# Second attention's value products in bursts of four key blocks, with six score banks and rows of three pairs

## The chip, the cores and the metric

The kernel runs on one core of a Trainium2 chip. The metric is the device time of one execution in microseconds; the median of the runs is compared. TensorE (PE) multiplies matrices, VectorE (DVE) and ScalarE (ACT) work element by element, GpSimd (POOL) does simple element work, and SyncE (SP) issues the DMAs. Each engine takes its own list of instructions in order and meets the others at semaphores.

## The reference

Sixteen sequences of 512 tokens with 128 features go through two layers. Each layer normalises, and adds an attention and a feed-forward product to its input:

```
xn = layernorm(x);  x = x + attn0(xn) + ffn0(xn)     # layer 0: 16 heads of 64, causal, with slopes
xn = layernorm(x);  x = x + attn1(xn) + ffn1(xn)     # layer 1: differential attention
# attn1, for each of 8 heads, with two query/key sets of 8 features and values of 16:
o1 = softmax(q1 k1^T * 8**-0.25) @ v;  o2 = softmax(q2 k2^T * 8**-0.25) @ v
o  = rmsnorm(o1 - lam * o2) * w + b;   attn1 = (1 - lambda_init) * concat(o) @ Wo^T
```

The change is in attn1's products `softmax(...) @ v`: 8 heads x 2 sets = 16 score sets, in 4 groups (`NG`) of 4 (`GS`), each over 4 key blocks of 128 (`NT`).

## The kernel before

All engines walk through the same clock of *ticks*. A sequence takes 32 ticks (`TICKS`), four for each of the first layer's 8 head pairs; what an engine does in a tick depends on the tick modulo 4 (`r`) and is an order written out by hand in each engine's `tick`. Each piece of work has a tick of its own (`FA_AT`, `WOB_AT`, ...). The first layer of one sequence runs beside the second layer of the sequence before: in a tick TensorE projects q, k or v of a pair, makes scores (`max_scores0`, L1500), turns probabilities (`turn_probs`, L1517) or multiplies them with the values (`pv0`, L1532), and between them it does *steps* of the second attention. There are 46 steps (`NU + KEY_LAG`) in 28 ticks, so one or two in a tick, its `part` 0 and 1.

A step of the second attention makes two score tiles for the row maxima (`second_tops`, L1605, read by DVE's `row_max1`, L1250) and, 14 steps later, two score tiles with the keys as rows (`second_keys`, L1591); ACT's `exp1` (L989) writes the exponentials of the latter to `pt1`. Two tiles are a *unit*; 8 units are a group. `pt1` holds two blocks of four tiles, used in turn. Every second step `second_values` runs `pv1` (L1552 to L1563) for one key block: 4 heads' matmuls, recorded as 8, into the bank `op`. After the fourth block ACT copies `op` to `oraw` (`copy_heads`, L973, at step 9 of the group's end), TensorE turns `oraw` (`turn_heads`, step 10), and DVE and POOL normalise (`head_norm_a`, `head_scale`, `head_norm_b`). The fourth group's last block, copy and turn have ticks of their own (`TAIL_AT`, `TURN3_AT`). In the clock modulo 32 the fourth blocks of the groups stand in ticks 7, 12, 17 and 22.

TensorE's eight result banks are two for projections (`pj`), five for scores (`sc`, `SCB`) and `op`. Projections of all kinds take the two `pj` banks in turn, in the order that `pj_order` lists; `bank` makes TensorE wait until the use two before has been read. Score tiles take the score banks in turn in the order of `score_order`; `bank_free` makes TensorE wait for the reader of the tile that had the bank. Tick 12 also holds `WOB_AT`: the second half of the first layer's output projection (L1548, 128 matmuls), and tick 13 begins with the last turning of a pair and its `pv0`.

The first layer's probabilities stand in `pq`, four pairs deep (`NROWS`); DVE writes a pair when the pair four before has been turned. In the last sequence parts of `pq` serve as the second attention's stacks, values and result.

Of the kernel before, what the change touches and what calls it, by code (L numbers as in the profile page):

```python
# [55 lines left out]
NROWS = 4  # L56
# [58 lines left out]
L1_TICKS = 28  # L115
# [28 lines left out]
KEY_LAG = 14  # L144
# [6 lines left out]
PV_LAG = (0, 0)  # L151
L1_STEPS = NU + KEY_LAG
SCB = 5


def l1_chunk(h, part=None):

    m = (h - L1_AT) % TICKS
    steps = range(L1_STEPS * m // L1_TICKS, L1_STEPS * (m + 1) // L1_TICKS) if m < L1_TICKS else range(0)
    return steps if part is None else steps[part:part + 1]  # L160
# [22 lines left out]
def l1_heads(t, at, last=NG - 1):  # L183

    g, r = divmod(t - KEY_LAG - at, GU)
    return g if r == 0 and 0 <= g < last else None
# [5 lines left out]
               (TURN3_AT, f"o{NG - 1}"), (OT_AT, "oT"), (OUT_AT, "wo1")]  # L192
# [3 lines left out]
class Seq:  # L196
# [21 lines left out]
    def live(self):  # L218

        return 0 <= self.lo < NB  # L220

# [23 lines left out]
def l1_steps(h, k, part=None):  # L245

    steps = []
    for n, clock in enumerate((h, k)):
        if clock is not None:
            i = Seq((clock - L1_AT) // TICKS)  # L250
            if i.live() and i.last() == (n == 1):
                steps.extend((i, t) for t in l1_chunk(clock, part))
    return steps
# [22 lines left out]
def pj_order():  # L276
# [3 lines left out]
    def second(h, k, part):  # L280

        for i, t in l1_steps(h, k, part):
            if (group := l1_rows(t)) is not None:
                order.append((f"n{group}", i.lo))
            if (group := l1_heads(t, TURN_AT[i.last()])) is not None:
                order.append((f"o{group}", i.lo))

# [11 lines left out]
    for g, h, k in clocks():  # L299
# [3 lines left out]
        if late(g) and r == 0:  # L303
# [4 lines left out]
            second(h, k, 1)  # L308
        elif late(g) and r == 1:
            pairs("pv", g, 3)  # L310
            second(h, k, 0)
            misc(g, h, k)
            second(h, k, 1)
        elif late(g) and r == 2:
# [3 lines left out]
            second(h, k, 1)  # L318
        elif late(g) and r == 3:
            second(h, k, 0)  # L320
            misc(g, h, k)
            second(h, k, 1)
        elif r == 0:
            pairs("q", g, -1)
            pairs("k", g, -1)
            second(h, k, 0)
            second(h, k, 1)
            misc(g, h, k)
        elif r == 1:
# [3 lines left out]
            misc(g, h, k)  # L333
        elif r == 2:
            second(h, k, 0)
            pairs("v", g, -1)
            misc(g, h, k)
            second(h, k, 1)
        else:
            second(h, k, 0)  # L340
            misc(g, h, k)
            second(h, k, 1)
# [3 lines left out]
def score_order():  # L346
# [3 lines left out]
    def second_keys(h, k, part):  # L350

        for i, t in l1_steps(h, k, part):
            if t >= KEY_LAG:
                order.extend(("st1", 2 * (t - KEY_LAG) + n, i.lo) for n in range(2))

# [128 lines left out]
def build_program(nc, a, out):  # L484
    ctx = ExitStack()
    with ctx:
# [73 lines left out]
        stacks = [(QS, KS), tuple(rows_of[n][:, 0:H1 * T // 2].bitcast(BF16).rearrange("p (n t) -> p n t", n=H1) for n in range(2))]  # L560
# [3 lines left out]
        result = [xres, rows_of[3][:, 0:NT * D].rearrange("p (t d) -> p t d", t=NT)]  # L564
        values1 = [v1, rows_of[2][:, 0:NT * H1 * 32].rearrange("p (t h e) -> p t h e", t=NT, h=H1)]
        pt1 = sb("pt1", [P, 2 * GS, T])
# [11 lines left out]
        ow = sb("ow", [P, NT, 2, DV])  # L578
# [4 lines left out]
        op = ps("op")  # L583
# [37 lines left out]
        s_or = sem("heads_copied")  # L621
# [9 lines left out]
        flat = pt1[:, :, :].rearrange("p a f -> p (a f)").rearrange("p (n f) -> p n f", f=2 * FF)  # L631
# [48 lines left out]
        def _(sp):  # L680
# [36 lines left out]
            def stack(i, w):  # L717
# [5 lines left out]
                if i.last():  # L723

                    sp.wait_ge(s_tr, i.upto(N_TURN, 6 * 6))
# [36 lines left out]
        def _(pool):  # L762
# [10 lines left out]
            def last_stacks(i):  # L773

                pool.wait_ge(s_tr, i.upto(N_TURN, 6 * 6))
                pool.memset(stacks[1][1][:, :, :], 1.0).then_inc(s_pset, 1)
                pool.wait_ge(s_tr, i.upto(N_TURN, 6 * 7))
# [31 lines left out]
            def scale_probs(i, p, q):  # L809

                for c in (2 * q, 2 * q + 1):
                    j, row = ROWS[c]
                    at = PT0 * (2 * (p % NROWS) + j) + ROW_OFF[row]
# [4 lines left out]
                    pool.tensor_scalar(rows, rows, rsum[:, p % NROWS, c:c + 1], None, ALU.mult).then_inc(s_scl, 1)  # L818
# [11 lines left out]
            def small(g, h, k):  # L830
# [6 lines left out]
                for i, t in l1_steps(h, k):  # L837
                    if (group := l1_heads(t, TURN_AT[i.last()] + SCALE_LAG[i.last()])) is not None:
# [40 lines left out]
        def _(act):  # L879
# [62 lines left out]
            def exp0(i, p, q):  # L942

                for c in (2 * q, 2 * q + 1):
                    j, row = ROWS[c]
                    at = PT0 * (2 * (p % NROWS) + j) + ROW_OFF[row]
                    rows = pq[:, at:at + P * (row + 1)]
                    act.wait_ge(s_mxd0, i.upto(L0N, 8 * p + c + 1))
                    act.activation(rows, rows, ACT.Exp, scale=-1.0, bias=mx0[:, p % NROWS, c:c + 1],  # L949
                                   accum_out=lsum[:, p % NROWS, c:c + 1]).then_inc(s_exp0, 1)  # L950
# [31 lines left out]
            def exp1(i, n):  # L982

                m, j = divmod(n, GS // 2)
                if j == 0:
                    hold(act, s_pv1, i.upto(NG * NT, m - 1))
                for h in range(2):
                    act.wait_ge(s_st1, i.upto(L1N, 2 * n + h + 1))
                    act.activation(pt1[:, GS * (m % 2) + 2 * j + h, :], sc[tile_bank(i, "st1", 2 * n + h)][:, :],  # L989
                                   ACT.Exp, scale=float(DS) ** -0.25).then_inc(s_exp1, 1)  # L990

            def second_attention(h, k, part):

                for i, t in l1_steps(h, k, part):
                    if (group := l1_rows(t)) is not None:
                        minus_max1(i, group)
                    if (group := l1_heads(t, HEADS_AT[i.last()])) is not None:
                        copy_heads(i, group)
                    if t >= KEY_LAG:
                        exp1(i, t - KEY_LAG)  # L1000

            def others(g, h, k):
# [12 lines left out]
                for i in second_at(h, k, VALS_AT):  # L1015
# [7 lines left out]
                    else:  # L1023
                        hold(act, s_pv1, i.upto(NG * NT, 0))
# [76 lines left out]
        def _(dve):  # L1101
# [80 lines left out]
            def row_max0(i, p, q):  # L1182
# [4 lines left out]
                for c in (2 * q, 2 * q + 1):  # L1187
# [3 lines left out]
                    at = PT0 * (2 * (p % NROWS) + j) + ROW_OFF[row]  # L1191
                    left = P if row == 1 else 0
                    scores_there = i.upto(6 * NPAIR, m + 1)
                    if i.first():
# [4 lines left out]
                                             op0=ALU.add, op1=ALU.min, accum_out=mx0[:, p % NROWS, c:c + 1]).then_inc(s_mxd0, 1)  # L1199

            def invert_sums(i, p, q):

                dve.wait_ge(s_exp0, i.upto(L0N, 8 * p + 2 * q + 2))
                dve.reciprocal(rsum[:, p % NROWS, 2 * q:2 * q + 2], lsum[:, p % NROWS, 2 * q:2 * q + 2]).then_inc(s_rc, 1)  # L1204
# [79 lines left out]
            def second_attention(h, k, part):  # L1284

                for i, t in l1_steps(h, k, part):
                    if (group := l1_rows(t)) is not None:
                        minus_max1_rest(i, group)
                    if (group := l1_heads(t, TURN_AT[i.last()] + NA_LAG[i.last()])) is not None:
# [546 lines left out]
```

## Time and profile before

| | |
|---|---|
| runs shown | 2510.09, 2512.21, 2514.51 us; median 2512.21 us |
| profiled execution | 2513.58 us, of which the span from the first to the last instruction is 2511.6 us |
| busy share of the span | PE 94%, PE weight loads 44%, DVE 74%, ACT 75%, POOL 57% |
| granted TensorE clock | 0.986 of full speed, mean |

The span has a start of some 170 us in which the first sequence has nothing beside it, 15 sequences whose second layer runs beside the next one's first, and an end from about 2400 us on. Times in the timeline are from the span's start. A busy PE is not PE at its peak, since matmuls overlap and their ends are modelled; so block costs are read from one start to the next.

### The profile page before, as it was taken

How to read it: one execution, taken by the hardware profiler on the slowest of the kernel's cores; microseconds unless marked ns; L12 is line 12 of the kernel's file. 1: busy time of each engine (PE TensorE's matmuls, PEld its weight loads, DVE VectorE, ACT ScalarE, POOL GpSimd, SP SyncE). 2: the span in 40 equal slices, each digit the busy share in tenths (PEclk: the TensorE clock that was granted, in tenths of full speed). 3: DMA queues.
4: the chain of work that ended last, by engine and by line, in shares of the span. 5: the costliest groups of instructions: out<-in, count | busy, mean ns of one | idle time of the engine just before them, and what ended most of it. 6: DMA issues, size and time to landing. Idle time of an engine off the chain costs nothing.

```text
span 2511.6 us, 81917 instructions
## 1 busy us (share of the span) xinstructions
PE 2370.6 (94%) x32896; PEld 1112.7 (44%) x32896; DVE 1856.1 (74%) x5637; ACT 1882.8 (75%) x4707; POOL 1430.7 (57%) x1356
## 2 busy tenths in 40 slices
PE   6999999999999999999999999999999999999886
PEld 2454444444444444444444444444444444444421
DVE  4558777777877778777777877778777776867675
ACT  4866787878778777787878778777787878778545
POOL 5866474665656556474665656556574655646311
PEclk8999999999999999999999999999999999999978
DMA  3002020200202002020200202002020200202020
GB/s 96 7 14 45 3 61 3 49 15 7 57 2 57 6 19 44 3 61 3 53 10 7 56 3 61 3 21 43 7 56 3 55 8 7 57 3 56 2 56 5
DMA packets 59944, 70.43 MB, mean 28 GB/s; under 512 B 11056, under 2 KB 55344, under 8 KB 56368
## 3 DMA queue, kind: packets, MB, share of 16 engines
q1 hardware_dynamic: 59568, 65.21, 11.5%
q8 instruction: 262, 4.29, 0.7%
q14 instruction: 114, 0.93, 0.1%
HBM read 35.04 MB, written 29.36 MB: 26 GB/s over the span
## 4 chain that ended last, share of the span: by engine, by line
PE 72%; ACT 14%; DVE 10%; issue 2%; DMA 1%; POOL 1%; SPq 0%; POOLq 0%; ACTq 0%; DVEq 0%
PE pj L1436 17%; PE pj L1532 10%; PE sc L1500 9%; PE op L1561 7%; PE sc L1517 7%; ACT pt L989 5%; PE pj L1548 5%; PE pj L1456 5%; DVE mx L1250 4%; PE sc L1605 4%; PE sc L1591 4%; ACT pq L949 3%; ACT pt L967 3%; PE pj L1426 3%; DVE pq L1197 2%
## 5 line engine op out<-in xcount | busy, mean ns | idle before, releaser
L818 POOL TENSOR_SCALAR pq<-pq,rsum 128x128 f32<-128x128 f32 (+3 forms) x1024 | 1130.5, 1121 | 743.0 <-DVE rsum L1204 742.6
L1250 DVE TENSOR_REDUCE mx<-sc 128x1 f32<-128x512 f32 x1024 | 655.9, 683 | 199.1 <-PE sc L1605 195.1
L989 ACT ACTIVATE pt<-sc 128x512 f32<-128x512 f32 x1024 | 556.3, 610 | 191.5 <-PE sc L1591 191.2
L949 ACT ACTIVATE pq<-pq,mx 128x128 f32<-128x128 f32 (+3 forms) x1024 | 573.2, 576 | 16.6 <-DVE mx L1197 16.6
L967 ACT ACTIVATE pt<-sc 128x512 f32<-128x512 f32 (+1 forms) x768 | 360.8, 538 | 221.2 <-PE sc L1517 217.7
L1197 DVE CUSTOM_DVE_ANT_0 pq<-sc,relkey 128x128 f32<-128x128 f32 (+3 forms) x1024 | 448.3, 484 | 104.9 <-PE sc L1500 100.0
L1500 PE MATMUL sc<-K,Q 64*128 64x128 f32 (+3 forms) x2048 | 365.5, 454 | 26.9 <-ACT pt L989 16.7
L1532 PE MATMUL pj<-pt,v 128*32 128x512 f32 (+3 forms) x4096 | 304.5, 438 | 3.9 <-ACT y L917 0.6
L1517 PEld LDWEIGHTS sc<-ident,pq 64*128 64x128 f32 x5120 | 199.2, 139 | 171.6 <-issue 127.3
L1436 PE MATMUL pj<-xnT,wqkv 128*32 128x512 f32 x2048 | 264.4, 609 | 7.6 <-DVE xres L1173 2.9
L1561 PE MATMUL op<-pt,v 128*32 128x512 f32 x1920 | 256.8, 607 | 2.2 <-ACT pt L989 2.0
L1517 PE MATMUL sc<-ident,pq 64*128 64x64 f32 x5120 | 234.8, 228 | 24.4 <-DVE mx L1197 12.8
L1500 PEld LDWEIGHTS sc<-K,Q 64*128 64x128 f32 x2048 | 159.8, 188 | 153.5 <-issue 133.6
L1605 PE MATMUL sc<-KS,QS 48*128 48x512 bf16 x960 | 210.2, 384 | 16.9 <-ACT pt L967 5.5
L949 ACT ACTIVATION_READ_ACCUMULATOR pq<-pq,mx 128x1 f32 x1024 | 220.1, 215 | 0.0
L1591 PE MATMUL sc<-QS,KS 51*128 51x512 bf16 x960 | 199.9, 386 | 6.0 <-ACT pt L967 4.2
L1532 PEld LDWEIGHTS pj<-pt,v 128*32 128x32 f32 x4096 | 126.1, 110 | 160.8 <-issue 134.2
L1591 PEld LDWEIGHTS sc<-QS,KS 51*128 51x128 bf16 x960 | 51.0, 94 | 226.4 <-issue 119.7
L1605 PEld LDWEIGHTS sc<-KS,QS 48*128 48x128 bf16 x960 | 58.0, 94 | 190.4 <-DVE mx L1250 60.6
L1436 PE MATMUL pj<-wqkv,xnT 128*32 128x128 f32 x4096 | 138.9, 276 | 0.0
L1436 PEld LDWEIGHTS pj<-wqkv,xnT 128*32 128x32 f32 x4096 | 104.6, 110 | 55.2 <-issue 52.0
L1204 DVE RECIPROCAL rsum<-lsum 128x2 f32<-128x2 f32 x512 | 79.4, 155 | 58.6 <-ACT pq L949 58.3
(117 smaller groups left out, 2798.2 us busy)
## 6 DMA issues: line engine op xcount, KB each, us to landing
scr_p<-y SPq DMA_DIRECT2D x160, 128.0 KB, 2.4
QS<-scr_p SPq DMA_DIRECT2D x30, 384.0 KB, 6.1
KS<-scr_p SPq DMA_DIRECT2D x30, 384.0 KB, 8.8
x_in<-in_L_attn_x SPq DMA_DIRECT2D x16, 256.0 KB, 2.8
scr_p<-tanh SPq DMA_DIRECT2D x32, 128.0 KB, 2.4
out_x<-xres SPq DMA_DIRECT2D x15, 256.0 KB, 2.3
QS<-nrow SPq DMA_DIRECT2D x180, 4.0 KB
wqkv<-in_L_attn_w_qkv SPq DMA_DIRECT2D x1, 1536.0 KB, 6.5
```

Source lines behind the costliest of these rows:

```text
L818: pool.tensor_scalar(rows, rows, rsum[:, p % NROWS, c:c + 1], None, ALU.mult).then_inc(s_scl, 1)
L949: act.activation(rows, rows, ACT.Exp, scale=-1.0, bias=mx0[:, p % NROWS, c:c + 1], accum_out=lsum[:, p % NROWS, c:c + 1]).then_inc(s_exp0, 1)
L967: act.activation(to[:, :, h, :], sc[tile_bank(i, "tr0", m)][:, 0:cols].rearrange("p (n c) -> p n c", c=HALF), ACT.Copy).then_inc(s_ev, 1)
L989: act.activation(pt1[:, GS * (m % 2) + 2 * j + h, :], sc[tile_bank(i, "st1", 2 * n + h)][:, :], ACT.Exp, scale=float(DS) ** -0.25).then_in ...
L1197: dve.tensor_tensor_reduce(out=pq[:, at:at + width], in0=sc[tile_bank(i, "mx0", m)][:, left:left + width], in1=relkey[:, T - width:T], sca ...
L1250: dve.reduce_max(mx1[:, g % 2, at:at + 1], sc[tile_bank(i, "mx1", 2 * t + h)][:, :], AXIS.X).then_inc(s_mxd1, 1)
L1436: last = pe.matmul(t[r, c * k:c * (k + 1)], w(k)[:, r], x(k), start=True, stop=True)
L1500: last = pe.matmul(sc[tile_bank(i, "mx0", m + j)][:, left:left + width], Q0[r, b, P * row:P * (row + 1)], K0[r, b, 0:width], start=True, s ...
L1517: last = pe.transpose(sc[tile_bank(i, "tr0", m + h)][:, HALF * n:HALF * (n + 1)], pq[r, at:at + P], ident[r, r])
L1532: last = pe.matmul(t[r, P * k:T], v0[:, p % NBUF, k, r], pt[:, base:base + WIDTH[k]], start=k == 0, stop=k == NT - 1)
L1561: last = pe.matmul(op[32 * j:32 * (j + 1), :], values1[i.last()][:, k, (GS * g + j) // 2, :], pt1[:, GS * (k % 2) + j, :], start=k == 0, s ...
L1605: pe.matmul(sc[tile_bank(i, "mx1", 2 * t + n)][:, :], queries[r, slot, P * q:P * (q + 1)], keys[r, slot, :], start=True, stop=True).then_i ...
```

## The change

`pv1` no longer runs block by block. It runs once for a group, at step 8 after the group's first keys (`VALUES_AT`; the place of the fourth block before), as one burst of four key blocks, into a `pj` bank under the name `w0` to `w3`; inside it TensorE waits before each block for that block's exponentials. `copy_heads` reads that `pj` bank. The bank `op` is gone and there are six score banks. `pt1` grows from 8 tiles to 9 units (18 tiles), used in turn through all sequences; `exp1` waits for the block that last read the unit. `NROWS` goes from 4 to 3, with pairs counted through all sequences (`row_slot`), `ow` becomes another name of `dif`, and the last sequence's stacks, values and result move to other rows. The orders of the engines' ticks stay; `pj_order` gets `values` where TensorE's order had `second_values`. `L1_TICKS` and `KEY_LAG` become pairs with the same values.

```diff
-NROWS = 4
+NROWS = 3
+UNITS = 9
-PV_LAG = (0, 0)
-SCB = 5
+VALUES_AT = (8, 8)
+SCB = 6
...
+def row_slot(i, p):
+    return i.upto(NPAIR, p) % NROWS
...
 SECOND_MISC = [..., (FB_AT, "fb"),
-               (TURN3_AT, f"o{NG - 1}"), ...]
+               (TAIL_AT, f"w{NG - 1}"), (TURN3_AT, f"o{NG - 1}"), ...]
...
+    def values(h, k, part):
+        for i, t in l1_steps(h, k, part):
+            if (group := l1_heads(i, t, VALUES_AT[i.last()])) is not None:
+                order.append((f"w{group}", i.lo))
...
         elif r == 0:
             pairs("q", g, -1)
             pairs("k", g, -1)
+            values(h, k, 0)
             second(h, k, 0)
+            values(h, k, 1)
             second(h, k, 1)
             misc(g, h, k)
...
-        pt1 = sb("pt1", [P, 2 * GS, T])
+        pt1 = sb("pt1", [P, 2 * UNITS, T])
-        ow = sb("ow", [P, NT, 2, DV])
+        ow = dif
-        op = ps("op")
...
             def copy_heads(i, g):
-                act.wait_ge(s_pv1, i.upto(NG * NT, NT * (g + 1)))
-                act.activation(oraw[:, :], op[:, :], ACT.Copy).then_inc(s_or, 1)
+                b, u = pj_use(i, f"w{g}")
+                act.wait_ge(s_pjf[b], u)
+                act.activation(oraw[:, :], pj[b][:, :], ACT.Copy).then_inc(s_pje[b], 1)
...
             def exp1(i, n):
-                m, j = divmod(n, GS // 2)
-                if j == 0:
-                    hold(act, s_pv1, i.upto(NG * NT, m - 1))
+                unit = i.upto(NU, n)
+                if unit >= UNITS:
+                    was, m = divmod((unit - UNITS) // (GS // 2), NG * NT)
+                    group, k = divmod(m, NT)
+                    if k < NT - 1:
+                        act.wait_ge(s_pv1, Seq(was).upto(NG * (NT - 1), (NT - 1) * group + k + 1))
+                    else:
+                        b, u = pj_use(Seq(was), f"w{group}")
+                        act.wait_ge(s_pjf[b], u)
...
-            def pv1(i, g, k):
-                pe.wait_ge(s_exp1, i.upto(L1N, GS * (NT * g + k + 1)))
-                if k == 0:
-                    hold(pe, s_or, i.upto(NG, g))
-                    ...
-                for j in range(GS):
-                    last = pe.matmul(op[32 * j:32 * (j + 1), :], values1[i.last()][:, k, (GS * g + j) // 2, :],
-                                     pt1[:, GS * (k % 2) + j, :], start=k == 0, stop=k == NT - 1)
-                last.then_inc(s_pv1, 1)
+            def pv1(i, g):
+                ...
+                t, full = bank(i, f"w{g}")
+                for k in range(NT):
+                    pe.wait_ge(s_exp1, i.upto(L1N, GS * (NT * g + k + 1)))
+                    for j in range(GS):
+                        unit = i.upto(NU, (GS * (NT * g + k) + j) // 2)
+                        last = pe.matmul(t[32 * j:32 * (j + 1), :], values1[i.last()][:, k, (GS * g + j) // 2, :],
+                                         pt1[:, 2 * (unit % UNITS) + j % 2, :], start=k == 0, stop=k == NT - 1)
+                    if k < NT - 1:
+                        last.then_inc(s_pv1, 1)
+                last.then_inc(full, 1)
...
             def second_values(h, k, part):
                 for i, t in l1_steps(h, k, part):
-                    m = t - KEY_LAG
-                    if m >= GS // 2 + PV_LAG[i.last()] and (m - PV_LAG[i.last()]) % (GS // 2) == 0:
-                        pv1(i, *divmod((m - PV_LAG[i.last()]) // (GS // 2) - 1, NT))
+                    if (group := l1_heads(i, t, VALUES_AT[i.last()])) is not None:
+                        pv1(i, group)
...
                 for i in second_at(h, k, TAIL_AT):
-                    pv1(i, NG - 1, NT - 1)
+                    pv1(i, NG - 1)
```

## Rows read from the trace of the kernel before

**Rows 1.** The page's first part: busy us (share of the span) x instructions, by engine.

```profile
PE 2370.6 (94%) x32896; PEld 1112.7 (44%) x32896; DVE 1856.1 (74%) x5637; ACT 1882.8 (75%) x4707; POOL 1430.7 (57%) x1356
```

**Rows 2.** The page's chain that ended last, by engine, by line.

```profile
PE 72%; ACT 14%; DVE 10%; issue 2%; DMA 1%; POOL 1%; SPq 0%; POOLq 0%; ACTq 0%; DVEq 0%
PE pj L1436 17%; PE pj L1532 10%; PE sc L1500 9%; PE op L1561 7%; PE sc L1517 7%; ACT pt L989 5%; PE pj L1548 5%; PE pj L1456 5%; DVE mx L1250 4%; PE sc L1605 4%; PE sc L1591 4%; ACT pq L949 3%; ACT pt L967 3%; PE pj L1426 3%; DVE pq L1197 2%
```

**Rows 3.** Windows: length, busy of PE, PEld, DVE, ACT, POOL, then clock, DMA.

```profile
1307.82:1323.35 15.53, 15.14 (x178) 5.55 (x176) 10.75 (x32) 13.78 (x36) 8.09 (x8) 1.00 0.01 2
1323.35:1350.61 27.26, 26.25 (x375) 12.26 (x373) 21.44 (x61) 21.23 (x53) 12.78 (x13) 1.00 0.01 3
1350.61:1355.11 4.50, 4.50 (x139) 3.70 (x138) 1.46 (x5) 0.59 (x2) 4.50 (x4) 1.00 0.02 4
1355.11:1375.88 20.77, 19.86 (x237) 8.77 (x234) 14.18 (x64) 19.14 (x51) 11.39 (x14) 1.00 0.05 16
1375.88:1397.43 21.55, 21.44 (x284) 9.12 (x286) 17.25 (x46) 18.59 (x48) 15.15 (x14) 1.00 0.24 66
1397.43:1458.25 60.82, 58.41 (x865) 29.52 (x857) 50.29 (x146) 43.92 (x110) 36.71 (x36) 1.00 0.19 36
sum 150.43, PE 145.60 PEld 68.91 DVE 115.36 ACT 117.26 POOL 88.63; mean PE 24.27 PEld 11.49 DVE 19.23 ACT 19.54 POOL 14.77
```

**Rows 4.** Groups by line, value matmuls: count, busy us, mean ns, idle before.

```profile
L1561 PE MATMUL op<-pt,v 128*32 128x512 f32 x1920 | 256.8, 607 | 2.2 <-ACT pt L989 2.0
```

**Rows 5.** Timeline of PE: start us, length us, line, tiles, count.

```profile
1215.96 1.92 PE L1436 MATMUL pj<-xnT,wqkv 128*32 128x512 f32 x16
1217.82 0.39 PE L1591 MATMUL sc<-QS,KS 51*128 51x512 bf16 x2
...
1393.38 0.39 PE L1591 MATMUL sc<-QS,KS 51*128 51x512 bf16 x2
1393.70 1.06 PE L1561 MATMUL op<-pt,v 128*32 128x512 f32 x8
1394.70 0.39 PE L1591 MATMUL sc<-QS,KS 51*128 51x512 bf16 x2
1394.92 0.81 PE L1500 MATMUL sc<-K,Q 64*128 64x384 f32 x4
```

**Rows 6.** Timeline of PE behind the second output projection; in brackets idle time before.

```profile
1355.11 0.39 PE L1591 MATMUL sc<-QS,KS 51*128 51x512 bf16 x2
...
1355.67 2.36 PE L1532 MATMUL pj<-pt,v 128*32 128x512 f32 x32
...
1359.21 0.92 PE L1500 MATMUL sc<-K,Q 64*128 64x384 f32 x4 [0.64 <-ACT pt L989]
```

**Rows 7.** Timeline of ACT in the same place.

```profile
1355.59 1.09 ACT L989 ACTIVATE pt<-sc 128x512 f32<-128x512 f32 x2 [4.38 <-PE sc L1591]
...
1357.96 0.61 ACT L973 ACTIVATE oraw<-op 128x512 f32<-128x512 f32 x1
1358.44 1.11 ACT L989 ACTIVATE pt<-sc 128x512 f32<-128x512 f32 x2
```

**Rows 8.** Windows of ACT alone inside stretches 2 and 4: length, busy, clock, DMA.

```profile
1332.80:1339.29 6.49, 6.32 (x17) 1.00 0.00 1
1355.59:1375.20 19.61, 18.46 (x49) 1.00 0.06 16
```

**Rows 9.** PE's waits from 1247 to 1308: us in total, times, longest (first and last).

```profile
PE sc L1500 <- DVE mx L1250: 0.7, 1, 0.7
...
PE pj L1436 <- DVE xres L1173: 0.2, 1, 0.2
```

**Rows 10.** Timeline of PE near 173 us, and the windows view just behind.

```profile
173.04 0.46 PE L1517 MATMUL sc<-ident,pq 64*128 64x64 f32 x8 [2.29 <-DVE mx L1197]
173.44 4.05 PE L1532 MATMUL pj<-pt,v 128*32 128x512 f32 x32
...
173.94:177.36 3.42, 3.42 (x32) 1.16 (x24) 0.90 (x7) 1.13 (x5) 3.42 (x4) 0.50 0.00 0
```

More of the change, by code:

```diff
@@ L150, with l1_chunk @@
 NA_LAG = (0, 0)
-PV_LAG = (0, 0)
-L1_STEPS = NU + KEY_LAG
-SCB = 5
-def l1_chunk(h, part=None):
+VALUES_AT = (8, 8)
+SCB = 6
+def l1_chunk(h, last, part=None):
     m = (h - L1_AT) % TICKS
-    steps = range(L1_STEPS * m // L1_TICKS, L1_STEPS * (m + 1) // L1_TICKS) if m < L1_TICKS else range(0)
+    ticks, all_steps = L1_TICKS[last], NU + KEY_LAG[last]
+    steps = range(all_steps * m // ticks, all_steps * (m + 1) // ticks) if m < ticks else range(0)
     return steps if part is None else steps[part:part + 1]
@@ L251, in l1_steps @@
             if i.live() and i.last() == (n == 1):
-                steps.extend((i, t) for t in l1_chunk(clock, part))
+                steps.extend((i, t) for t in l1_chunk(clock, n, part))
     return steps
@@ L352, in second_keys @@
         for i, t in l1_steps(h, k, part):
-            if t >= KEY_LAG:
-                order.extend(("st1", 2 * (t - KEY_LAG) + n, i.lo) for n in range(2))
+            if t >= KEY_LAG[i.last()]:
+                order.extend(("st1", 2 * (t - KEY_LAG[i.last()]) + n, i.lo) for n in range(2))
     def second_tops(h, k, part):
@@ L837, in small @@
                 for i, t in l1_steps(h, k):
-                    if (group := l1_heads(t, TURN_AT[i.last()] + SCALE_LAG[i.last()])) is not None:
+                    if (group := l1_heads(i, t, TURN_AT[i.last()] + SCALE_LAG[i.last()])) is not None:
                         head_scale(i, group)
@@ L996, in second_attention @@
                         minus_max1(i, group)
-                    if (group := l1_heads(t, HEADS_AT[i.last()])) is not None:
+                    if (group := l1_heads(i, t, HEADS_AT[i.last()])) is not None:
                         copy_heads(i, group)
-                    if t >= KEY_LAG:
-                        exp1(i, t - KEY_LAG)
+                    if t >= KEY_LAG[i.last()]:
+                        exp1(i, t - KEY_LAG[i.last()])
             def others(g, h, k):
@@ L1288, in second_attention @@
                         minus_max1_rest(i, group)
[L1289 removed]
+                    if (group := l1_heads(i, t, TURN_AT[i.last()] + NA_LAG[i.last()])) is not None:
                         head_norm_a(i, group)
[L1291 removed]
+                    if (group := l1_heads(i, t, TURN_AT[i.last()] + NORM_LAG[i.last()])) is not None:
                         head_norm_b(i, group)
@@ L1576, in second_turns @@
                         pe.transpose(rows[0:16, 0:P], mx1[:, group % 2, 0:16], ident[:, :]).then_inc(full, 1)
-                    if (group := l1_heads(t, TURN_AT[i.last()])) is not None:
+                    if (group := l1_heads(i, t, TURN_AT[i.last()])) is not None:
                         turn_heads(i, group)
```

77 lines of the change are left out of this document (46 added, 31 removed).

## The prediction

> **What bounds the kernel now.** I read the busy line first: TensorE 94% of the span, ACT and DVE 75% each [rows 1]. That alone would say that any time taken off TensorE comes off the end. The chain of waits says less: 72% of the span runs over TensorE, 14% over ACT, 10% over DVE, and the value matmuls (L1561) hold 7% of it, 176 us, where they are busy 257 us in 15 of the 16 sequences alone [rows 2, 4]. About a third of their time is beside the path already. So I cut one steady sequence (150.43 us) into six stretches at the value blocks that the change touches and read which engine has room in each [rows 3]: TensorE has none anywhere, but ACT is busy 13.78 of 15.53 us in stretch 1, 19.14 of 20.77 in stretch 4 and 18.59 of 21.55 in stretch 5. Inside them it runs without a break: 6.32 of 6.49 us and 18.46 of 19.61 us [rows 8]. In such places a shorter TensorE only waits for ACT.
>
> **The sum, per sequence.** There are 15 sequences of this shape: 1920 matmuls by 8 a block are 240 blocks, 16 each [rows 4]. The sixteenth sequence, at the end, is priced by itself.
>
> *What a block and a burst cost.* A block of 8 matmuls takes 1.00 us from its start to the next start, and the key scores in front of it take 0.32 instead of 0.22, so a removed block is worth 1.10. Sixteen matmuls of the same kind in a row take 1.86, so each further eight costs 0.86 [rows 5]. A burst is then 1.00 + 3 x 0.86 = 3.58 us where its last block was 1.00: 2.58 longer. By TensorE alone a sequence gains 12 x 1.10 = 13.2 and pays 4 x 2.58 = 10.3: 2.9 us. Between the four parts of a burst stands a wait for exponentials; if each part paid a full 1.00 again, a burst would be 0.42 longer (1.7 us a sequence).
> The Trainium skill ("TensorEngine Tiling (Array Packing)", Key Properties) says that a change of tiling mode drains the engine; by that rule the 2.9 us would simply be gained, which is the first rival below. The same page (PSUM Bottleneck) warns that packing speeds up TensorE but not the emptying of its banks; ACT's rows bear that out here.
>
> *Stretch 1 (1307.82 to 1323.35), three blocks gone.* TensorE alone: -3.3. ACT's idle time is 1.75, and the burst must wait for the exponentials of its last unit, behind that same ACT queue. Between 0 and -1.75; I take -1.2, nearer to ACT's end, since TensorE's own saving is twice that.
>
> *Stretch 2 (to 1350.61), a burst in, three blocks gone.* +2.6. The two blocks ahead of the first FFN's second product lie where ACT runs 6.32 of 6.49 us on end [rows 8] and the next key scores need banks that ACT still reads; I let them give 1.1 of 2.2. The third stands before DVE work and gives its 1.1. Net +0.4, between -0.7 (all given) and +2.6.
>
> *Stretch 3 (to 1355.11), a burst in.* The group's last block is followed at once by the 128 matmuls of the output projection; ACT works 0.59 us in it [rows 3], nothing covers it: +2.6.
>
> *Stretch 4 (to 1375.88), the new wait.* The projection banks are handed out in turn, two of them. In this tick the uses become q, k, **w1** (the burst), woB, and then pv of the next tick, so pv needs the bank of w1, that is, ACT's copy_heads. Before, its bank was k's. TensorE reaches pv at 1355.67, right after woB [rows 6]; but ACT gets to copy_heads only at 1357.96 and ends it at 1358.57, because ahead of it in ACT's queue stand the exponentials whose keys TensorE issues after woB (1355.59), the two turned copies and the first layer's exponentials [rows 7]. TensorE stops for 2.9 us, and queued behind pv are the key scores that ACT takes next (1357.96, now some 2.9 later): both engines lose it. The three blocks of this stretch cannot pay for it: ACT's work cannot shrink and its idle time is 19.61 - 18.46 = 1.15 [rows 8], of which I let 0.7 go, since the next pv comes behind ACT's copies again. So +2.2, between +1.75 and +2.9.
>
> *Stretch 5 (to 1397.43), a burst in, three blocks gone.* TensorE alone +2.6 - 3.3 = -0.7; ACT has 2.96 us of room [rows 3], but its copy now waits for the end of the burst: I take -0.6, between -0.7 and +1.
>
> *Stretch 6 (to 1458.25), a burst in and the sixth score bank alone.* +2.6 for the last group's burst. TensorE's six waits in the same place one sequence before, from 0.7 for DVE's maxima to 0.2 for DVE's residual, make 1.9 [rows 9]; with one tile more in the ring each asks for the reader of a tile earlier, so I count them all gone, though one is for a projection bank: +0.7, between +0.7 and +2.6, or lower if shorter stalls inside blocks go too (to -1).
>
> Together -1.2 + 0.4 + 2.6 + 2.2 - 0.6 + 0.7 = **+4.1 us** a sequence, some 60 us over 15 (61.5, less a little for the first and last of them, whose neighbours differ).
>
> *Edits that I cost at nothing.* Rows of three pairs: DVE's first scores of a pair now wait for the turning of the pair three before it, which program order has 3 ticks earlier, 3 x 150.43 / 32 = 14 us [rows 3]; that is the cover, and without it the price is a DVE wait of what is missing. Nine units of pt1: a unit needs the buffer of the one nine before, first at step 9, where ACT already waits for the whole burst in copy_heads. In the last sequence copy_heads comes a step later and that wait stands alone; there ACT also loses its keys during a burst but has no value blocks between its units; I put its tail at 0, between -5 and +5 us (two bursts' 2.6 either way). ow in dif: both are DVE's, in order. SP's and POOL's waits on turned pairs move in the last sequence alone, to pairs turned 5 ticks or more before; the number of DMAs is the same. After w0 the next use, q, takes the bank of ya3, which is empty by then; k takes w0's and waits for its copy a little, which is inside stretch 2's bounds.
>
> The profiled execution took 2513.6 us; 2513.6 + 60 = 2573.6. The median of the runs shown is 1.4 lower, so I forecast **2572 us**.
>
> **Rivals.**
> *TensorE alone decides (faster).* Its 94% and 72% speak for it. Then every removed block counts: -2.9, the sixth bank -1.9, and pv's wait +2.9, which no bank order here removes: -1.9 a sequence, 28 us, **2484 us**. It decides where ACT's queue would be more than 2 us ahead of TensorE in stretches 1, 2 and 4; rows 8 speak against it. That ACT could reach copy_heads before woB ends, so that pv does not wait at all, would add 2.9 (2440 us); exponentials whose keys come after woB stand before it, so I give that almost nothing.
> *The clock falls after the new wait (slower still).* After TensorE stood still for 2.29 us at 173.04, pv0's 32 matmuls took 4.05 us instead of 2.36, at a granted clock of 0.50, which is 1.2 GHz [rows 6, 10]. The new wait is longer than that one and pv follows it. That costs up to 1.7 more a sequence, 25 us: **2597 us**. Against it: it is one row, and not every sequence need meet it.
> The Trainium skill ("TensorE: Matmul & The Clock Gate", Part 1) says that the engine's default state is the throttled one and that activity releases it; the row agrees.
> *The gains and the waits cancel.* If stretches 1 and 2 give what their bounds allow (-1.75 and -0.7) and stretch 6 gives -1, the sum is +1.5, and 1.5 us more from stretch 4 or 5 would make it nothing: **2512 us**.
>
> **How the numbers follow.** Forecast 0.52 (its own range 2545 to 2595), clock 0.20, TensorE alone 0.18, cancelled 0.10. A difference under 0.2%, 5 us, is no change here. The cancelled case splits about evenly over faster, same and slower, and the others fall on their sides: faster 0.20, same 0.06, slower 0.74. The range takes in the clock case with part of the burst's bound (2615) above, and below it the better ends of stretches 1, 2 and 6, which reach to 2505; about 0.13 of the chance lies under it and 0.06 above.
>
> **What would show it.** Right: a wait of some 2.9 us on TensorE before L1532 for ACT's copy into oraw, once in a sequence, and as long an idle time on ACT before the next key exponentials; bursts of 32 matmuls of 3.5 to 3.6 us; the 0.64 us wait of L1500 for L989 behind pv gone [rows 6]; TensorE's busy time some 45 us lower (15 x 2.9) while its idle time grows by some 100; ACT's busy time unchanged. Wrong: a wait for that copy under 1 us; stretch 4 no longer than before; or TensorE's idle time not above its 2511.6 - 2370.6 = 141 us [rows 1]. If bursts take 4.0 us, the price of a part was wrong, not the reason.

## The result, and the profile after

| | before | after |
|---|---|---|
| median of 4 runs, us | 2511.15 (2507.31 to 2514.51) | 2625.36 (2623.81 to 2630.20) |
| ratio | | 1.0459, 95% interval 1.0438 to 1.0479 |
| span of the profiled execution, us | 2511.6 | 2623.7 |
| granted TensorE clock, mean | 0.986 | 0.974 |

The change makes the kernel 4.6% slower. The direction and the new wait came as forecast; the time did not: 2625 lies 10 us above the range and 53 above the forecast.

The page's busy line and chain of the kernel after, to be read beside [rows 1, 2]:

```profile
PE 2383.2 (91%) x32896; PEld 1163.5 (44%) x32896; DVE 1848.2 (70%) x5637; ACT 1870.9 (71%) x4707; POOL 1426.6 (54%) x1356
PE 67%; ACT 17%; DVE 10%; issue 4%; POOL 1%; DMA 0%; SPq 0%; POOLq 0%; ACTq 0%; DVEq 0%
```

ACT's and DVE's busy times are within 12 us of those before. TensorE's idle time went from 141 to 240 us, as forecast (some 100 more). Its busy time did not fall by 45 us, it rose by 13. The chain now runs 17% over ACT. Where TensorE waits (whole run: us in total, times, longest; the first five rows of after):

```profile
PE pj L1568 <- ACT oraw L1000: 41.7, 14, 3.0
PE sc L1553 <- ACT pt L1023: 23.0, 28, 1.5
PE pj L1598 <- ACT v L960: 17.4, 14, 1.2
PE sc L1631 <- DVE mx L1233: 13.2, 43, 0.7
PE pj L1472 <- ACT Q L949: 12.4, 14, 0.9
```

The first row is the predicted one (2.98 us each, 2.9 forecast). The third, group 3's burst waiting for ACT's copy of v, was not predicted. The second is new in its length: before, the same turns (L1517) waited 28 times for these exponentials, 0.2 us at the longest and 5.9 in all, while 16.7 us of waits for them stood before L1500; those are gone. One sequence of after in windows (length, busy of PE, PEld, DVE, ACT, POOL, clock, DMA), from group 3's burst of the sequence before: stretches 6 and 1 together, then 2, 3, 4 and 5 of [rows 3]:

```profile
1288.12:1364.00 75.88, 72.77 (x1034) 35.83 (x1034) 61.09 (x177) 56.76 (x143) 44.75 (x43) 1.00 0.15 29
1364.00:1391.59 27.59, 26.45 (x375) 12.81 (x374) 20.97 (x61) 20.83 (x53) 12.39 (x13) 1.00 0.01 3
1391.59:1398.65 7.06, 7.06 (x160) 4.47 (x161) 1.44 (x5) 0.92 (x2) 5.50 (x4) 1.00 0.01 2
1398.65:1423.51 24.86, 19.25 (x213) 9.56 (x210) 14.16 (x65) 19.07 (x51) 10.30 (x13) 0.93 0.04 13
1423.51:1446.55 23.04, 20.91 (x283) 9.43 (x283) 17.24 (x46) 19.03 (x49) 15.36 (x14) 1.00 0.20 54
sum 158.43, PE 146.44 PEld 72.10 DVE 114.90 ACT 116.61 POOL 88.30; mean PE 29.29 PEld 14.42 DVE 22.98 ACT 23.32 POOL 17.66
```

Nearly all the growth is in stretches 3 to 5, and stretch 4 alone has a clock below 1. TensorE's and then ACT's timeline there (start, length, line, tiles; in brackets idle time before and what ended it), where [rows 6, 7] stood before:

```profile
1391.59 3.64 PE L1598 MATMUL pj<-pt,v 128*32 128x512 f32 x32 [0.19 <-ACT Q L949]
1395.04 3.68 PE L1584 MATMUL pj<-wout,att 128*32 128x128 f32 x128
1398.65 0.39 PE L1631 MATMUL sc<-QS,KS 51*128 51x512 bf16 x2
1398.88 0.41 PE L1553 MATMUL sc<-ident,pq 64*128 64x64 f32 x8
1402.26 4.05 PE L1568 MATMUL pj<-pt,v 128*32 128x512 f32 x32 [2.98 <-ACT oraw L1000]
1406.25 0.39 PE L1631 MATMUL sc<-QS,KS 51*128 51x512 bf16 x2
...
1406.69 0.81 PE L1536 MATMUL sc<-K,Q 64*128 64x384 f32 x4
```

```profile
1399.14 1.09 ACT L1023 ACTIVATE pt<-sc 128x512 f32<-128x512 f32 x2 [6.63 <-PE sc L1631]
...
1401.51 0.61 ACT L1000 ACTIVATE oraw<-pj 128x512 f32<-128x512 f32 x1
1406.73 1.08 ACT L1023 ACTIVATE pt<-sc 128x512 f32<-128x512 f32 x2 [4.61 <-PE sc L1631]
```

The burst takes 3.45 us from its start to the next start. `pv0` stands 2.98 us until ACT's copy, which stands behind exponentials whose keys came after the output projection, and ACT then idles 4.61 us for its next keys. The 0.64-us wait of [rows 6] is gone. `pv0` itself takes 4.05 us instead of 2.36, at half the clock (1.2 GHz), as a window inside it shows:

```profile
1402.73:1406.14 3.41, 3.41 (x32) 1.51 (x24) 0.00 (x0) 0.00 (x0) 0.00 (x0) 0.50 0.00 0
```

And in stretch 5, the wait that was missed, with the projection before it:

```profile
1437.40 1.92 PE L1472 MATMUL pj<-xnT,w_l 128*32 128x512 f32 x16 [0.89 <-ACT Q L949]
...
1446.55 3.64 PE L1598 MATMUL pj<-pt,v 128*32 128x512 f32 x32 [1.24 <-ACT v L960]
```

Over twelve steady sequences (the second to the thirteenth), from burst start to burst start (medians, us):

| stretch | before | after | change | forecast |
|---|---|---|---|---|
| 6 and 1 | 76.38 | 75.89 | -0.5 | -0.5 |
| 2 | 27.01 | 27.60 | +0.6 | +0.4 |
| 3 | 4.49 | 7.07 | +2.6 | +2.6 |
| 4, clock at 1.00 (4 of 12) | 20.77 | 23.16 | +2.4 | +2.2 |
| 4, clock at 0.50 in part (8 of 12) | 20.77 | 24.3 to 25.5 | +3.6 to +4.8 | (a rival) |
| 5 | 21.55 | 23.04 | +1.5 | -0.6 |

### The profile page after: what moved, and what is told of

Its sections match the earlier page's. It is cut to its first block, busy times and chain, and to the rows that moved or that the text cites. A ratio compares the mean times of both kernels' runs of the same rounds, so it can differ in the third digit from the quotient of the medians.

```text
span 2623.7 us, 82166 instructions
## 1 busy us (share of the span) xinstructions
PE 2383.2 (91%) x32896; PEld 1163.5 (44%) x32896; DVE 1848.2 (70%) x5637; ACT 1870.9 (71%) x4707; POOL 1426.6 (54%) x1356
## 4 chain that ended last, share of the span: by engine, by line
PE 67%; ACT 17%; DVE 10%; issue 4%; POOL 1%; DMA 0%; SPq 0%; POOLq 0%; ACTq 0%; DVEq 0%
PE pj L1472 16%; PE pj L1568 12%; PE pj L1598 9%; ACT pt L1023 9%; PE sc L1536 6%; PE sc L1553 5%; DVE mx L1286 5%; PE pj L1584 5%; PE pj L1492 4%; PE sc L1631 4%; PE sc L1645 4%; ACT pq L975 4%; PE pj L1462 2%; ACT pt L993 2%; DVE pq L1233 2%
## 5 line engine op out<-in xcount | busy, mean ns | idle before, releaser
L1568 PE MATMUL pj<-pt,v 128*32 128x512 f32 (+3 forms) x4096 | 321.4, 457 | 44.4 <-ACT oraw L1000 41.7
L1598 PE MATMUL pj<-pt,v 128*32 128x512 f32 x1920 | 218.4, 595 | 25.5 <-ACT v L960 17.4
L1631 PE MATMUL sc<-QS,KS 51*128 51x512 bf16 x960 | 217.7, 386 | 18.8 <-DVE mx L1233 13.2
L1568 PEld LDWEIGHTS pj<-pt,v 128*32 128x32 f32 x4096 | 134.6, 114 | 210.1 <-issue 182.2
L813 POOL TENSOR_SCALAR veps<-mv 128x4 f32<-128x4 f32 x64 | 15.0, 234 | 240.0 <-DVE mv L1186 236.2
L851 POOL TENSOR_SCALAR mse<-ms 128x8 f32<-128x8 f32 x64 | 13.1, 205 | 227.8 <-DVE ms L1304 225.4
```

The lines of the kernel that those rows point to most:

```text
L1568: last = pe.matmul(t[r, P * k:T], v0[:, p % NBUF, k, r], pt[:, base:base + WIDTH[k]], start=k == 0, stop=k == NT - 1)
L1598: last = pe.matmul(t[32 * j:32 * (j + 1), :], values1[i.last()][:, k, (GS * g + j) // 2, :], pt1[:, 2 * (unit % UNITS) + j % 2, :], start= ...
L1631: pe.matmul(sc[tile_bank(i, "st1", 2 * m + n)][:, :], keys[r, slot, P * k:P * (k + 1)], queries[r, slot, :], start=True, stop=True).then_i ...
```

## The experiments

My theory on seeing this: three terms make up the miss, the wait for v's copy, the clock behind the new wait, and something small at the end. Rivals: ScalarE is late whatever task asks (then a wait removed turns up elsewhere); the clock falls for another reason; the bursts cost more by themselves than the forecast allowed, and the sixth bank covers it. Times are medians; the kernel before took 2511.8 to 2512.6 in the same batches.

**E1, group 1's copy one step earlier.**

```diff
-HEADS_AT = (9, 10)
+HEADS_AT = ((9, 8, 9), 10)
```

> Only edit to the changed kernel: ScalarE's copy of group 1's sums stands one step earlier in its queue, ahead of the exponentials of step 30 instead of behind them (all else as in the changed kernel, 2625.4 us). Theory A (the 2.98-us wait of layer 0's value product for that copy, 14 times, plus the granted clock of 0.5 that follows it in 9 of 15 sequences at about 2 us each): the wait goes in all sequences and so do the 0.5 stretches behind it; 14 x 2.98 = 42, 9 x 2 = 18, so 55 to 62 us less, about 2567. Theory B (the clock falls for another reason): 42 us less, about 2583, and the 0.5 stretches stay. Theory C (ScalarE is late anyway, the copy only changes what is late): under 15 us less, and a wait of like length on the next row of ScalarE's.

Measured 2562.1 us, 63 less than the kernel after (ratio to before 1.0203, 1.0188 to 1.0218). Theory A. TensorE and ACT of E1 in the same place:

```profile
1519.19 3.68 PE L1587 MATMUL pj<-wout,att 128*32 128x128 f32 x128
1522.80 0.39 PE L1634 MATMUL sc<-QS,KS 51*128 51x512 bf16 x2
1523.02 0.41 PE L1556 MATMUL sc<-ident,pq 64*128 64x64 f32 x8
1523.36 2.36 PE L1571 MATMUL pj<-pt,v 128*32 128x512 f32 x32
```

```profile
1519.44 0.60 ACT L1003 ACTIVATE oraw<-pj 128x512 f32<-128x512 f32 x1 [2.79 <-PE pj L1601]
1523.28 1.08 ACT L1026 ACTIVATE pt<-sc 128x512 f32<-128x512 f32 x2 [3.25 <-PE sc L1634]
```

The copy now runs beside the output projection, `pv0` starts at once and takes 2.36 us. Stretch 4 is 20.11 us in all twelve sequences, and from 180 to 2360 us the clock is 1.00 throughout, where after has nine stretches at 0.50, 41 us in all.

**E2, group 3's burst ahead of the next sequence's values** (TensorE's order and the banks' order; 14 sequences), and **E3, both edits.**

```diff
+        order.extend((f"w{NG - 1}", i.lo) for i in second_at(h, k, TAIL_AT) if i.lo < NB - 2)
         order.extend((name, i.lo) for tick, name in SECOND_MISC for i in second_at(h, k, tick)
+                     if not (tick == TAIL_AT and i.lo < NB - 2))
```

> Only edit to the changed kernel: in the tick that holds both, the burst of group 3 stands ahead of the next sequence's projection of values (in TensorE's order and in the banks' order), in 14 of 16 sequences; so the burst gets the bank that ScalarE empties first. Theory A (the burst waits 1.24 us for ScalarE's copy of v, 14 times): that wait goes, 14 to 19 us less, about 2608. Theory C (ScalarE is what is late, whichever task asks): the wait turns up on the next bank, within 4 us of the changed kernel's 2625.

> Both edits together (copy of group 1 one step earlier, burst of group 3 ahead of the values' projection). Theory A: the sum of the two, 70 to 80 us less than 2625, about 2550; what is left over the kernel before is the burst that TensorE runs at once ahead of layer 0's output (2.58 us per sequence, 39 us in 15), less the gains of the other stretches. Theory C: less than 60, because ScalarE's lateness moves from the one place to the other.

E2: 2607.95 us, 17 less (1.0382, 1.0366 to 1.0397). E3: 2546.9 us, 78.5 less (1.0138, 1.0123 to 1.0153); the two add up (63 + 17), so theory C falls. The burst's idle time, after and then E2 (groups by line: count, busy, mean ns, idle before):

```profile
L1598 PE MATMUL pj<-pt,v 128*32 128x512 f32 x1920 | 218.4, 595 | 25.5 <-ACT v L960 17.4 <-ACT Q L949 2.6 <-ACT att L966 2.3
```

```profile
L1600 PE MATMUL pj<-pt,v 128*32 128x512 f32 x1920 | 218.4, 595 | 8.3 <-ACT Q L951 2.6 <-ACT att L968 2.3 <-ACT y L945 1.8
```

E3's sequence, in the windows of after. Group 3's burst now starts earlier, which moves 1.2 us from stretch 5 to the next 6; against before, stretches 5, 6 and 1 together are 0.2 shorter, stretch 4 is 0.7 shorter, and what is left is 2.6 in stretch 3 and 0.6 in stretch 2:

```profile
1399.25:1476.30 77.05, 73.53 (x1073) 36.75 (x1065) 63.45 (x184) 59.10 (x150) 47.29 (x45) 1.00 0.17 35
1476.30:1503.89 27.59, 26.45 (x374) 12.79 (x373) 20.99 (x63) 20.83 (x53) 12.39 (x13) 1.00 0.01 3
1503.89:1510.96 7.07, 7.07 (x161) 4.48 (x162) 1.34 (x5) 1.52 (x3) 5.50 (x4) 1.00 0.03 7
1510.96:1531.08 20.12, 17.49 (x214) 8.75 (x210) 14.17 (x65) 18.58 (x50) 10.30 (x13) 1.00 0.05 15
1531.08:1551.79 20.71, 19.82 (x250) 8.59 (x250) 14.98 (x39) 16.70 (x42) 13.03 (x12) 1.00 0.17 46
sum 152.54, PE 144.35 PEld 71.35 DVE 114.94 ACT 116.73 POOL 88.52; mean PE 28.87 PEld 14.27 DVE 22.99 ACT 23.35 POOL 17.70
```

**E4, five score banks.** The edit is `SCB = 5`.

> Only edit to the changed kernel: five score banks instead of six, so one bank of PSUM is left unused. By the prediction's term (the sixth bank takes 1.9 us of waits for the row maxima out of each sequence): 25 to 31 us more than 2625, about 2654. Rival (the waits are VectorE's own pace, a bank more only defers them): within 5 us of 2625.

Measured 2707.8 us (1.0776, 1.0758 to 1.0794): 82 more, not 28. Stretches 6 and 1 are 1.93 us longer, the forecast's 1.9 to the hundredth; but stretch 2 is 1.5 longer at full clock and 3.0 where the clock falls there too, which the forecast had not booked for the bank. From 180 to 2360 us the clock is at 0.50 in 17 places, where after has nine, so a part of the 82 is the clock's.

**E5, the wait filled.** Twelve matmuls ahead of the waiting `pv0`, into the score bank that the next keys write.

```diff
+                    filler(h, k)
                     p, i = pair(g, 3)
                     if i is not None:
                         pv0(i, p)
...
+    bank_free(i, "st1", 2 * m)
+    for n in range(12):
+        pe.matmul(sc[tile_bank(i, "st1", 2 * m)][:, :], keys[...], queries[...], start=True, stop=True)
```

> The changed kernel with twelve more matmuls (51x512, bf16, of which one took 0.2 us in a row of its trace) ahead of layer 0's value product that waits 2.98 us for the copy, 14 or 15 times; their sums are written over and used by nothing. Theory A (TensorE standing idle in that wait is what brings the granted clock of 0.5, and the clock costs 1.7 to 2.35 us in 9 sequences beyond the wait): TensorE is busy for 2.6 of the 2.98 us, the 0.5 stretches go, stretch 4 is 23.2 us in every sequence, 15 to 21 us less than 2625, about 2607. Theory B (the clock falls for another reason, or those sequences are longer for another reason): the 0.5 stretches stay, within 4 us of 2625, or more where the added matmuls reach past the wait.

Measured 2608.3 us (1.0384, 1.0369 to 1.0400), 17 less with more work on TensorE. Theory A:

```profile
920.68 0.39 PE L1631 MATMUL sc<-QS,KS 51*128 51x512 bf16 x2
920.91 0.41 PE L1553 MATMUL sc<-ident,pq 64*128 64x64 f32 x8
921.15 2.75 PE L1643 MATMUL sc<-QS,KS 51*128 51x512 bf16 x12
924.30 2.36 PE L1568 MATMUL pj<-pt,v 128*32 128x512 f32 x32 [0.39 <-ACT oraw L1000]
```

`pv0` is 2.36 us and stretch 4 is 23.17 us in 11 of 12 sequences; in the twelfth the clock fell 16 us later, behind another wait (1.5 us, for exponentials), and once more it fell in a stretch 2. So the idle time of `pv0`'s wait brought the clock down, and the clock cost 17 us.

**E6, the output projection ahead of group 1's burst** (on top of E3; the cut shows TensorE's order, the banks' order moves with it), and **E7, that burst one step later** (on top of E2).

```diff
                     second_turns(h, k, 1)
                     others(g, h, k)
+                    second_values(h, k, 1)
                     second_keys(h, k, 1)
```

```diff
-VALUES_AT = (8, 8)
+VALUES_AT = ((8, 9, 8), 8)
-HEADS_AT = (9, 10)
+HEADS_AT = ((9, 10, 9), 10)
```

> As both edits together (2547), and group 1's burst stands behind the second half of layer 0's output projection instead of ahead of it. Theory A (the output projection's lateness of 2.58 us is passed on through VectorE's addition and norm to what TensorE does next): 2.6 x 15 = 39 us less, about 2508. Theory B (TensorE has enough other work between, and only its own sum counts): within 8 us of 2547, and the next value product may wait some tenths of a us for VectorE's addition, whose bank it now gets.

> The changed kernel with group 3's burst ahead of the values' projection, and group 1's burst and copy one step later (step 31 in place of 30, behind the value product of layer 0); so the value product doesn't follow that burst in the banks. Theory A: as in the run with both edits, about 2547, less what the output projection gains by standing ahead of the burst (up to 39 us). Rival: the exponentials of step 31 now need a slot that this burst has yet to free (nine pairs of slots), ScalarE stands behind it, and the gain is eaten: 2555 to 2575.

E6: 2550.2 us (1.0154, 1.0139 to 1.0169); E7: 2556.1 us (1.0176, 1.0159 to 1.0193). Neither gains over E3: the 2.58 us are not the output projection's lateness. E7's sequences are 152.4 us, as E3's, or about 154.1; in the second kind the clock fell behind a wait of 1.6 us:

```profile
1530.95 0.46 PE L1558 MATMUL sc<-ident,pq 64*128 64x64 f32 x8 [1.59 <-ACT pt L1028]
1531.52 3.63 PE L1573 MATMUL pj<-pt,v 128*32 128x512 f32 x32
```

E7's time lies in its rival's range, and the rival's wait is there: ACT's exponentials wait 15 times for the burst, 23.2 us in all, and never in E3. But at full clock its sequences are no longer than E3's; the six sequences with the clock at 0.50, 1.6 us each, make most of E7's 9 us over E3.

**E8, the bursts alone:** into a bank `op` of their own, five score banks.

```diff
-SCB = 6
+SCB = 5
+        op = ps("op")
...
-                t, full = bank(i, f"w{g}")
+                hold(pe, s_or, i.upto(NG, g))
+                t, full = op, s_opf
```

> The bursts alone: the bursts of four key blocks and the rows of three as in the changed kernel, but into a PSUM bank of their own as in the kernel before, and five score banks as before. By the prediction's terms without the new bank wait (2.9) and without the sixth bank (1.9): about 4.1 - 2.9 + 1.9 = 3.1 us per sequence over the kernel before, 2512 + 46 = 2558. By subtraction from the run with five banks (2708) of what the two bank waits gave (63 and 17): about 2628, so that the bursts alone would cost some 115 us, and the bank handed to the scores would be worth 82 us by itself.

Measured 2630.4 us (1.0470, 1.0454 to 1.0485): the subtraction holds, the forecast's terms don't. Where TensorE waits in E8:

```profile
PE sc L1536 <- ACT pt L1024: 35.7, 56, 0.7
PE sc L1553 <- ACT pt L1024: 29.3, 69, 1.1
PE sc L1553 <- DVE mx L1233: 29.0, 39, 2.3
PE sc L1645 <- DVE mx L1286: 14.8, 57, 0.8
```

All of TensorE's listed waits before products into score banks together are 77 us before, 160 in E8, 80 in E3 (5 to 9 us of each are for a DMA or POOL, not for a bank). Most sequences of E8 are 156.9 to 157.1 us, the shortest 6.7 over before: +1.4 in stretches 6 and 1 (the forecast's -0.5 and the bank's 1.9), +2.1 in 2, +2.6 in 3, -0.3 in 4, +0.9 in 5.

**E9, keys of step 30 ahead of group 1's burst** (on top of E2; the line moves those of steps 17 and 43, in two other ticks, as well); **E10, between burst and output projection** (on top of E3); **E13, E9 with group 3's copy ahead of the values' copy; E12, the kernel before with rows of three alone.**

```diff
                     second_tops(h, k, 1)
+                    second_keys(h, k, 1)
                     second_values(h, k, 1)
                     second_turns(h, k, 1)
                     others(g, h, k)
-                    second_keys(h, k, 1)
```

> As the changed kernel with group 3's burst ahead of the values' projection (2608), and in the tick of group 1's burst the two key products of step 30 stand ahead of the burst instead of behind the output projection; group 1's copy stays where the changed kernel has it. It then stands behind the exponentials of step 30, which have their keys early. Theory A (in the run with both edits ScalarE stood idle 2.8 us in the burst and 3.3 us in the output projection for want of keys, and this is what the 2.58 us of stretch 3 still cost): the wait for the copy goes as in the run with both edits, 2547, and 1 to 2.6 us more per sequence, 2508 to 2532. Theory B (only TensorE's own work and the waits on other engines count, ScalarE's idle time there is made up later): 2543 to 2550.

> As the run with both edits (2547), and the keys of step 30 stand between group 1's burst and the output projection, so that ScalarE has them 3.5 us earlier. Theory A: half of the idle time is filled, 0.6 to 1.5 us per sequence less, 2525 to 2538. Theory B: 2543 to 2550.

> As the run with the keys first, and ScalarE's copy of group 3's sums stands ahead of its copy of the values (in 14 sequences). In the run with both edits a turn of layer 1 waited 6.1 us in all for that copy. Expected: 0 to 6 us less than the run with the keys first.

> The kernel before with rows of three pairs in place of four, and nothing else of the change. The prediction costed it at nothing, since the rows of a pair are turned and free well before VectorE writes the pair three later: within 5 us of 2512. Rival: VectorE's row maxima wait for the turns of three pairs before, some tenths of a us per pair, 128 pairs, 25 us or more on top.

E9: 2596.3 us (1.0327, 1.0310 to 1.0343), a miss of the design: ACT's copy stood behind turned copies that come after the output projection, and the wait was 2.22 us, as TensorE's and ACT's rows of E9 show:

```profile
1545.04 3.89 PE L1570 MATMUL pj<-pt,v 128*32 128x512 f32 x32 [2.22 <-ACT oraw L1002]
```

```profile
1535.60 1.15 ACT L1025 ACTIVATE pt<-sc 128x512 f32<-128x512 f32 x2
1542.88 0.66 ACT L995 ACTIVATE pt<-sc 128x256 f32<-128x256 f32 x2 [6.14 <-PE sc L1555]
...
1544.30 0.59 ACT L1002 ACTIVATE oraw<-pj 128x512 f32<-128x512 f32 x1
```

E13 stays there: 2597.3 us (1.0323, 1.0303 to 1.0343). E10: 2550.4 us (1.0146, 1.0131 to 1.0161), theory B. E12: 2511.1 us (0.9995, 0.9985 to 1.0004): the rows of three cost nothing.

**E14, E9 with the copy directly behind step 30's exponentials; E15, E14 with the keys of step 31 ahead of `pv0`; E16, E3 with the latter alone.** The cut is the edit of E15 and E16. It holds in every tick of that kind: besides step 31's it moves the keys of steps 18, 24, 37 and 44.

```diff
                     second_turns(h, k, 0)
+                    second_keys(h, k, 0)
                     p, i = pair(g, 3)
                     if i is not None:
                         pv0(i, p)
-                    second_keys(h, k, 0)
```

> As the run with both edits (2547), with the keys of step 30 ahead of group 1's burst and group 1's copy directly behind that step's exponentials (in the run with the keys first it stood behind copies of turned rows, which come after the output projection, and 2.2 us of the wait were back). Theory A (ScalarE's want of keys in burst and output projection, 6.0 us together, is what the remaining 2.2 us per sequence come from): of the 6.0 only about 0.5 to 1.1 can be filled by one pair of keys, so 8 to 16 us less, 2531 to 2539. Theory B (TensorE's own sum and other waits): 2543 to 2551.

> As the run before this, and in every tick of the second kind TensorE's keys of its first step stand ahead of layer 0's value product (2.36 us) instead of behind it. Theory A: ScalarE gets that pair of exponentials 2.4 us earlier, behind the output projection above all, and the 1.53-us wait of a turn for exponentials some 12 us later shrinks: 10 to 35 us less than the run before this. Theory B: within 5 us of it.

> As the run with both edits (2547), and only the keys of ticks of the second kind ahead of layer 0's value product (those of step 30 where the changed kernel has them). Theory A: 5 to 30 us less than 2547. Theory B: within 5 us of 2547.

E14: 2549.5 us (1.0152, 1.0137 to 1.0168), theory B. E15: 2543.2 (1.0129, 1.0112 to 1.0146) and E16: 2541.0 (1.0119, 1.0102 to 1.0136), each 6 us less than its neighbour (E14 and E3): E15 between its two theories, E16 at the near end of theory A's range. E16 is the fastest version with bursts, and still slower than the kernel before.

The clock hides a part of the gain. At full clock a sequence is 1.1 us shorter in E15 (151.6) and 0.9 in E16 (151.6); 0.7 of it lies in stretches 6 and 1 and only 0.1 to 0.2 in stretch 4. The keys now wait longer for DVE's row maxima, E3 and then E16:

```profile
PE sc L1636 <- DVE mx L1238: 12.3, 43, 0.5
```

```profile
PE sc L1636 <- DVE mx L1238: 21.3, 57, 0.9
```

Behind such a wait, or one of 1.0 to 1.1 us for exponentials a little later, the clock fell in nine steady sequences of E15 and eight of E16, at 0.3 to 1.8 us each; in E14 it fell in one, in E3 in none.

## Why the prediction was wrong

The runs make this account (us):

| | time | step |
|---|---|---|
| before; the same with rows of three | 2512; 2511 | 0 |
| bursts alone, own bank, five score banks (E8) | 2630 | +118 |
| into a projection bank, five score banks (E4) | 2708 | +77 |
| sixth score bank (after) | 2625 | -82, part of it the clock's |
| without the wait for group 1's copy (E1) | 2562 | -63: 42 the waits themselves, 17 the clock (E5), the rest open |
| and without the wait for v's copy (E3) | 2547 | -15 |

*Right.* The wait of `pv0` for the copy: 2.98 us measured, 2.9 forecast, for the reason given; without it stretch 4 is 0.7 shorter than before (E1), as the sum allowed. Stretch 3: 2.58. Stretches 6 and 1, which can't be told apart in after: -0.5 together, with the sixth bank's 1.9 in it (E4: 1.93). Rows of three at nothing (E12). Nine units at nothing: in after no exponential has a listed wait for a burst.

*The step that failed first: stretch 5.* The forecast followed the banks through the tick of group 1 and not through that of group 3. There the uses are v, vals, w3, so the burst gets v's bank and waits 1.24 us for ACT's copy; the layer-1 projection two uses behind q waits 0.89 us more for ACT's copy of Q. The step had "-0.6, between -0.7 and +1" and measured +1.5. E2 takes out the first of the two waits and 17 us.

*The clock was a rival and should have been a term.* It had 0.20 as a case of its own and 25 us; it happened in 9 sequences, and E5 prices it at 17 us. The one row it rested on [rows 10] was a wait shorter than the one forecast; that the longer one would meet it at least sometimes was the likelier reading. The Trainium skill ("TensorE: Matmul & The Clock Gate", Part 1) says that the throttled state is the default and activity releases it; E5 agrees: the same wait, filled with work, leaves the clock at 1.00.

*The ends.* The forecast had 0 there. The start up to the first sequence's last burst took 3.2 us less, the stretch from the last sequence but one's last burst to the end 7.7 more.

In numbers, by spans: forecast 61.5, measured 112.1. Stretch 5 is 2.1 x 14 = 29 of the difference, the clock 17 (E5), the ends 7.7 - 3.2 = 4.5; that makes 51, and the difference is 50.6. So close a fit is partly luck: stretches 2 and 4 came out 0.2 over each, the forecast counted 15 sequences where 14 lie between the ends, and these nearly cancel. (The cases' own chances, 0.10 split evenly, would give 0.21, 0.03 and 0.75 for faster, same and slower, not 0.20, 0.06 and 0.74.)

*What was right by chance.* Stretch 2 was forecast at +0.4 and came at +0.6, but without the sixth bank it is +2.1 (E8), and the bank's 1.5 there was not in the sum. E8 shows what the bursts do: with the blocks gone from between the score products, TensorE's listed waits for score banks double (77 to 160 us), and the sixth bank buys these back (80). I read it so: while TensorE ran a block, DVE and ACT emptied score banks.

"A removed block is worth 1.10" did not come off TensorE's sum: by windows its own work in a sequence fell from 145.60 to 144.35 (E3), 1.25 instead of 2.9. The groups by line tell where the rest went. The value matmuls' busy time fell from 256.8 us [rows 4] to 218.4, 2.6 a sequence, near the forecast. The key products' grew by 17.9, 1.2 a sequence (before, then E3):

```profile
L1591 PE MATMUL sc<-QS,KS 51*128 51x512 bf16 x960 | 199.9, 386 | 6.0 <-ACT pt L967 4.2 <-DVE mx L1250 0.9 <-ACT pt L989 0.7
```

```profile
L1636 PE MATMUL sc<-QS,KS 51*128 51x512 bf16 x960 | 217.8, 384 | 18.4 <-DVE mx L1238 12.3 <-ACT pt L1028 1.4 <-DMA QS<-nrow 0.6
```

One product still takes 0.38 us. What changed is that the two products of a step start together less often: the second waits for its bank. While the first runs this counts as busy, and the 0.10 us that mostly remain are not listed as a wait. The second starts more than 0.15 us late in 95 of the 480 pairs of E3, against 37 before; 62 of the 95 wait for ACT's exponentials, against 5. So the listed waits leave out a part of what the missing blocks cost, and the sixth bank does not buy all of it back. The Trainium skill ("TensorEngine Tiling (Array Packing)", Key Properties) has each change of tiling mode drain the engine, by which all 2.9 would have been gained; the trace gives 2.6 in the value matmuls and 1.25 in the sum.

*Open.* E3 is still 35 us behind the kernel before. Its listed waits before matmuls into projection banks are 86 us against 39 (and 7 for `op`), and its busy time is 16 us lower; that two banks now serve the bursts as well would explain it, but no run shows it: E10 took the 12.4 us of waits for Q away and gained nothing. That ACT starves in burst and output projection is not shown as a cause either: with the keys moved ahead stretch 4 is only 0.1 to 0.2 us shorter at full clock (E15, E16), but a new wait for DVE stands in it. What the late pairs of key products cost was read from the trace and not tried.

## What to carry to other kernels

When a result moves into banks that are handed out in turn, write down the order of uses for every tick in which it appears, and name for each use the engine and the queue place that empties the bank before; one tick was followed here and the other came out 29 us over its forecast. Work that stands between products of another kind may be a cover for the engines that empty their banks: price its removal with the wait that appears, not with its own length. A copy that frees a bank belongs directly behind what it copies, ahead of work whose inputs come later (E1: one step, 63 us).

## What the hardware showed that was not expected

The clock did not fall behind the 2.98-us wait every time. In after it fell in nine of 14 sequences, in E2, which keeps this wait, in 13 of 14. In the other sequences of after the same wait was followed by full speed, as in this row of after:

```profile
929.68 2.36 PE L1568 MATMUL pj<-pt,v 128*32 128x512 f32 x32 [2.98 <-ACT oraw L1000]
```

And in E7 a wait of 1.59 us was followed by half the clock in six sequences and by full speed in the others; in E16 it fell in six behind a wait of 0.94 us. So identical waits have two prices, and one row of a trace can't tell how often the dearer is paid; TensorE's idle time in front of dense work was worth filling even with work that is thrown away (E5, 17 us).
